# First-stage loads on a semaphore of their own, the first norm ahead of the table casts, the stack memsets at two bodies' ends

## What is computed

```python
x = L0_attn_x
x = x + _L0_attn_ref(_layernorm(x), W_in, W_out)      # q, k, v; clip; T_n(q), T_n(k); cumsum(T_n(k) v); num/den; @ W_out.T
x = x + _L0_ffn_ref(_layernorm(x), ln1_g, ..., exp_b2)

# inside _L0_ffn_ref
x = x + _attention(_layernorm(x, ln1_g, ln1_b), Wq, bq, Wk, bk, Wv, bv, Wp, bp)   # 16 heads, causal softmax
x = x + _token_moe(_layernorm(x, ln2_g, ln2_b), gate_W, gate_b, exp_W1, exp_b1, exp_W2, exp_b2)
```

## Time and profile before

| | us |
|---|---|
| median of 3 runs | 1512.45 (1511.88 to 1514.55) |
| the profiled execution | 1512.91 |
| its span | 1510.7 |
| PE busy | 1260.2 (83%) |
| DVE busy | 1167.6 (77%) |
| ACT busy | 918.9 (61%) |
| POOL busy | 854.2 (57%) |

### The profile page before, as it was taken

One profiled execution on the slowest core, in us unless ns is written; L12 is line 12 of the kernel. 1 busy time (PEld: TensorE's weight loads), 2 busy tenths in 40 slices (PEclk: granted clock), 3 DMA queues, 4 the chain that ended last, 5 costly groups with the idle time before them and its releaser, 6 DMA issues.

```text
span 1510.7 us, 27693 instructions
## 1 busy us (share of the span) xinstructions
PE 1260.2 (83%) x8757; PEld 722.4 (48%) x8819; DVE 1167.6 (77%) x2654; ACT 918.9 (61%) x1794; POOL 854.2 (57%) x1077
## 2 busy tenths in 40 slices
PE   2545898999989999998999999989888199999970
PEld 0222354544545454454544545444445178888850
DVE  4548789888998988889898898875551578888864
ACT  1131376666767667675666766666545289999950
POOL 5567445766676666656766666552032326666660
PEclk9666799999999999999999999999999589999995
DMA  3012321404223141321403214043143022222238
GB/s 97 0 49 36 85 64 23 103 20 107 65 51 86 30 112 50 67 79 37 110 21 92 75 34 100 16 100 86 30 135 134 30 76 77 86 86 81 81 134 333
DMA packets 79345, 116.23 MB, mean 77 GB/s; under 512 B 15396, under 2 KB 61496, under 8 KB 74976
## 3 DMA queue, kind: packets, MB, share of 16 engines
q1 hardware_dynamic: 65888, 92.41, 23.4%
q0 software_dynamic: 9088, 17.33, 3.4%
q10 hardware_dynamic: 4224, 4.72, 1.0%
HBM read 58.29 MB, written 57.43 MB: 77 GB/s over the span
## 4 chain that ended last, share of the span: by engine, by line
PE 61%; DVE 18%; issue 7%; ACT 6%; DMA 4%; POOL 3%; SPq 1%; POOLq 0%; DVEq 0%; another core or an unknown queue 0%; ACTq 0%
DVE nm L580 9%; PE scores L1386 8%; PE front L1547 7%; PE back L1406 7%; PE back L1559 7%; PE maxima L1360 7%; PE front L1289 3%; PE front L1264 3%; ACT pr L963 3%; PE scores L1389 2%; PE back L1243 2%; PE maxima L1362 2%; DMA stack<-pairs 2%; DVE front L531 1%; PE front L1338 1%
## 5 line engine op out<-in xcount | busy, mean ns | idle before, releaser
L580 DVE TENSOR_REDUCE nm<-maxima 128x1 f32<-128x384 f32 (+3 forms) x704 | 427.7, 634 | 94.1 <-PE maxima L1362 67.3
L963 ACT ACTIVATE pr<-scores 128x384 f32<-128x384 f32 (+1 forms) x768 | 378.5, 524 | 186.4 <-PE scores L1389 172.3
L1360 PE MATMUL maxima<-stack 96*128 96x128 bf16 (+3 forms) x1024 | 258.2, 311 | 43.1 <-DVE nm L580 33.2
L1386 PE MATMUL scores<-stack 98*128 98x512 bf16 (+3 forms) x1024 | 260.7, 310 | 33.7 <-ACT pr L963 27.8
L1386 PEld LDWEIGHTS scores<-stack 98*128 98x128 bf16 x1024 | 91.7, 101 | 205.6 <-ACT pr L963 134.1
L1389 PE MATMUL scores<-maskB,identb 128*128 128x128 bf16 (+1 forms) x768 | 186.4, 243 | 0.0
L1406 PE MATMUL back<-pr,vaug 128*9 128x512 f32 (+3 forms) x2048 | 183.2, 454 | 0.0
L1164 POOL DMA_INDIRECT xg<-rows,sloti x128 | 129.9, 1014 | 88.4 <-DVE sloti L653 47.0
L1134 POOL TENSOR_TENSOR kv<-F,kv 128x512 f32<-128x512 f32 x80 | 112.5, 1418 | 116.2 <-DVE kv L534 116.2
L1360 PEld LDWEIGHTS maxima<-stack 96*128 96x128 bf16 x1024 | 85.8, 99 | 169.1 <-DVE nm L580 113.4
L1232 POOL DMA_INDIRECT pairs<-xs x104 | 111.0, 1067 | 78.8 <-DVE xs L814 52.0
(11 more groups left out here) (223 smaller groups left out, 2491.7 us busy)
## 6 DMA issues: line engine op xcount, KB each, us to landing
stack<-spread SPq DMA_DIRECT2D x64, 384.0 KB, 6.4
spread<-qs SPq DMA_DIRECT2D x96, 128.0 KB
spread<-ks SPq DMA_DIRECT2D x96, 128.0 KB
xs<-xg SPq DMA_DIRECT2D x39, 272.0 KB, 2.9
stack<-pairs SPq DMA_DIRECT2D x8, 1024.0 KB, 16.6
xg<-xs SPq DMA_DIRECT2D x17, 272.0 KB
xs<-in_x SPq DMA_DIRECT2D x16, 256.0 KB, 5.8
acc<-xs SPq DMA_DIRECT2D x16, 256.0 KB, 2.3
```

The source lines that it names most:

```text
L580: v.tensor_reduce(nm[:, h:h + heads, t], ring(n)[:, 0:heads * (t + 1) * P].rearrange("p (h n) -> p h n", h=heads), AX.X, ALU.max, negate=T ...
L963: a.activation(pr[:, n % PR, 0:width], ringE[n % 2][:, 0:width], ACT.Exp).then_inc(W.exp_ready, 1)
L1360: k.matmul(ring(n)[:, at:at + (t + 1) * P], qst[p][0:MROW, h, t * P:(t + 1) * P], kst[p][0:MROW, h, 0:(t + 1) * P], start=(j == 0), stop=T ...
L1386: k.matmul(dst[:, at:at + T - t * P], kst[p][0:MROW + 2, h, t * P:(t + 1) * P], qst[p][0:MROW + 2, h, t * P:T], start=(t == tiles[0]), sto ...
```

## The change

The loads are split. `first_loads` (cst, w_in_sb, col) come right behind x of batch 0 and count on `f_loaded`; the nine others follow on `w_loaded`. The casts and tables move from before the loop into `set_tables`, which DVE runs behind the first norm's applies in body 0. The bias product moves to the end of body 0, as `add_bias` on DVE and `value_bias` on PE. ACT runs an activation of one column before it waits for the first loads, and waits for the other loads at the end of body 0. POOL sets stack buffer 0 at the end of body 0 and buffer 1 at the end of body 1, and SP waits for the pair that it is about to load.

```diff
-            loads = [(cst, consts[:, 0:C_KEPT]), (masks, consts[:, C_KEPT:C_N]), (col, cols), (row, row_biases), (w_in_sb, w_in),
-                     (wo_sb, w_out), (wq_sb, wq), (wk_sb, wk), (wv_sb, wv), (wp_sb, wp), (gw_sb, gate_w)]
+            first_loads = [(cst, consts[:, 0:C_KEPT]), (w_in_sb, w_in), (col, cols)]
+            loads = [(masks, consts[:, C_KEPT:C_N]), (row, row_biases), (wo_sb, w_out), (wq_sb, wq), (wk_sb, wk), (wv_sb, wv), (wp_sb, wp), (gw_sb, gate_w)]
             load_x(0)
+            for dst, src in first_loads:
+                sp.dma_start(dst[:, :], src).then_inc(W.f_loaded, 16)
...
-                    if g == 0:
-                        sp.wait_ge(W.stack_set, 4)
+                    if g < 2:
+                        sp.wait_ge(W.stack_set, 2 * g + 2)
...
-            dve.wait_ge(W.w_loaded, 16 * 12)
-            v.tensor_copy(identb[:, :], ident)
...
+            def set_tables():
+                dve.wait_ge(W.f_loaded, 16 * 3)
+                dve.wait_ge(W.w_loaded, 16 * 9)
+                v.tensor_copy(identb[:, :], ident)
...
+                v.tensor_scalar(bqs[:, :], col[:, V_BQ:V_BQ + 1], SCALE, None, ALU.mult).then_inc(W.const_ready, 1)
+            def add_bias():
+                dve.wait_ge(W.bp_step, 1)
+                v.tensor_copy(kv[:, 1, 0:D], X[:, 0:D]).then_inc(W.bp_step, 1)
+                dve.wait_ge(W.bp_step, 3)
+                v.tensor_tensor(row[:, R_BP:R_BP + D], X[:, 0:D], row[:, R_BP:R_BP + D], ALU.add).then_inc(W.bp_step, 1)
...
                     if at(17, f):
                         apply0(f)
+                        if f == 0:
+                            set_tables()
...
+                if f == 0:
+                    add_bias()
...
-            act.wait_ge(W.const_ready, 4)
-            act.wait_ge(W.w_loaded, 16 * 12)
+            act.wait_ge(W.const_ready, 1)
+            a.activation(warm[:, :], one[:, :], ACT.Copy)
+            act.wait_ge(W.f_loaded, 16 * 3)
...
+                if f == 0:
+                    act.wait_ge(W.const_ready, 4)
+                    act.wait_ge(W.w_loaded, 16 * 9)
...
-                if f == 0:
-                    for i in range(2):
-                        g_.memset(qst[i].rearrange("p h n -> p (h n)").bitcast(F32), 0.0).then_inc(W.stack_set, 1)
-                        g_.memset(kst[i].rearrange("p h n -> p (h n)").bitcast(F32), TWO_ONES).then_inc(W.stack_set, 1)
...
+                if f in (0, 1):
+                    g_.memset(qst[f].rearrange("p h n -> p (h n)").bitcast(F32), 0.0).then_inc(W.stack_set, 1)
+                    g_.memset(kst[f].rearrange("p h n -> p (h n)").bitcast(F32), TWO_ONES).then_inc(W.stack_set, 1)
...
-            pe.wait_ge(W.w_loaded, 16 * 12)
-            k.transpose(X[:, 0:D], row[:, R_BV:R_BV + D], ident).then_inc(W.bp_step, 1)
...
+            pe.wait_ge(W.f_loaded, 16 * 3)
+            def value_bias():
+                pe.wait_ge(W.w_loaded, 16 * 9)
+                pe.wait_ge(W.hq_ev, 1)
+                k.transpose(X[:, 0:D], row[:, R_BV:R_BV + D], ident).then_inc(W.bp_step, 1)
...
+                if f == 0:
+                    value_bias()
```

More of the change, by code:

```diff
@@ L262, in block_kernel @@
         names = """
-            bp_step stack_set w_loaded e_loaded const_ready pool_const tr0
+            bp_step stack_set f_loaded w_loaded e_loaded const_ready pool_const tr0
             h_taken hq_mm hk_mm hv_mm hk_ev hq_ev hv_ev k_clip q_clip k_sq q_sq k_t35 q_t35 k_t24 q_t24
@@ L473, in _ @@
             v.memset(vaug[:, :, :, :, DH:DH + 1], 1.0).then_inc(W.const_ready, 1)
-            dve.wait_ge(W.w_loaded, 16 * 12)
-            v.tensor_copy(identb[:, :], ident)
[L476 to L491, removed]
+            def set_tables():
+                dve.wait_ge(W.f_loaded, 16 * 3)
+                dve.wait_ge(W.w_loaded, 16 * 9)
+                v.tensor_copy(identb[:, :], ident)
+                v.tensor_copy(maskA[:, :].rearrange("p (h n) -> p h n", h=4), masks[:, 0:P].unsqueeze(1).to_broadcast((P, 4, P)))
+                v.tensor_copy(maskB[:, :].rearrange("p (i n) -> p i n", i=2), masks[:, P:2 * P].unsqueeze(1).to_broadcast((P, 2, P)))
+                v.tensor_copy(triu[:, :], masks[:, 2 * P:3 * P])
+                v.memset(onesb[:, :], 1.0)
+                v.tensor_copy(filled_to[:, :], cst[:, C_RG:C_RG + E])
+                v.memset(rows[:, :, :, D:RW], 0.0).then_inc(W.meta_ready, 1)
+                dve.wait_ge(W.meta_ready, 1)
+                v.tensor_copy(rowsi[:, :, :, R_ID], cst[:, C_TK:C_TK + 2 * QT].rearrange("p (k t) -> p k t", k=2)).then_inc(W.meta_ready, 1)
+                v.memset(fill, 0.0).then_inc(W.p_step, 1)
+                dve.wait_ge(W.p_step, 1)
+                v.tensor_copy(fill.rearrange("p (t c) -> p t c", t=QT)[:, :, R_ID].bitcast(U32), cst[:, C_DU:C_DU + QT]).then_inc(W.fill_ready, 1)
+                v.tensor_scalar(bqs[:, :], col[:, V_BQ:V_BQ + 1], SCALE, None, ALU.mult).then_inc(W.const_ready, 1)
@@ L1244, in turn @@
                 last.then_inc(done, 1)
-            pe.wait_ge(W.w_loaded, 16 * 12)
-            k.transpose(X[:, 0:D], row[:, R_BV:R_BV + D], ident).then_inc(W.bp_step, 1)
[L1248 to L1251, removed]
+            pe.wait_ge(W.f_loaded, 16 * 3)
[3 more added lines that the diff above has]
+                k.transpose(X[:, 0:D], row[:, R_BV:R_BV + D], ident).then_inc(W.bp_step, 1)
+                pe.wait_ge(W.bp_step, 2)
+                k.matmul(X[:, 0:D], kv[:, 1, 0:D], wp_sb[:, :], start=True, stop=True).then_inc(W.bp_step, 1)
+                pe.wait_ge(W.bp_step, 4)
+                pe.wait_ge(W.const_ready, 4)
             def turn_h(f, h, g):
```

## The result

Over 14 runs of each the changed kernel takes 1504.09 us (median) against 1512.01. The ratio is 0.9951 with a 95% interval of 0.9941 to 0.9962, so 5.7 to 8.9 us faster, 7.4 in the middle. 6.8 was forecast. The profiled execution took 1504.77 with a span of 1502.5, 8.2 shorter than before. One run, of 1590.97 us at a granted clock of 0.791 where the others have 0.909 to 0.916, is left out of the ratio.

What follows compares the result with a forecast made beforehand. Bound by a chain of single-instruction waits up to the first stack load, not throughput. 14.7 - 0.1 - 0.85 - 6.9 = 6.8 us off, forecast 1506.0 us; own range 1504.4 to 1508.5, 8 in 10 1502.8 to 1510.2.

Steps and rivals of the forecast that it cites:

- Start of the norm: Front of the kernel: first norm's statistics wait for x alone, at 3.8 in place of 17.18; gain 13.4 us.
- Table load: Prologue: a tiny ACT activation takes the table load at 24.01 off the chain before hT; gain 1.3 us.
- Tables and bias product: Body 0: tables hidden before the clip, cost nothing; bias product at the body's end delays PE's head sums, cost 0.1 us.
- TensorE's clock: Whole kernel: uncertainty; a matmul group on the other clock level moves the end by up to 1.7 us either way.
- First pair: POOL's memsets before the second norm's root: mostly covered, applies slower beside three POOL products; cost 0.85 us.
- Second pair: POOL's memsets before the root of norm 2, where DVE idles: nothing covers them, cost the full 6.9 us.
- products blocked: Rival at the first memsets: DVE's two-input products wait them out; 3.2 us lost, gain 4.4, 1508.5 us; chance 0.15.
- Stretched memsets: Rival at both pairs: memsets last longer among working engines; at 7 us each, slower at 1519 us; chance 0.07.
- The table load on the chain: Rival at ACT's start: the table load stays on the chain; gain 5.5 us, 1507.4 us; chance 0.04.
- The clock: Rival in the first bodies: two groups of ten fall to TensorE's lower level, 3.4 us lost, 1509.5 us; chance 0.12.

Runs made afterwards that it cites:

- memsets only: The kernel before with only POOL's four stack memsets moved to the ends of bodies 0 and 1; ratio to the kernel before 1.0005 (0.9991 to 1.0018).

## Why the prediction held

- Start of the norm: forecast 3.8, measured 3.52, because x landed after 2.7 us where the old trace had 3.0. hT at 10.35 for 10.6. This term was 0.25 short.
- Table load: 1.3 in the sum, 1.19 to 1.26 alone.
- Tables and bias product: the tables are hidden, as worked out. PE's head sums were released by DVE's bias add (ended 22.05) and not by POOL, and started at 22.33, 15.6 ahead of before where POOL's step was 15.8 ahead: 0.25 late where the sum has 0.1. None of it reached the chain, since DVE then waited for the root.
- TensorE's clock was named as the uncertainty and helped in body 0, which is luck and not part of the mechanism: the projections took 4.47 in place of 5.49, which put 0.9 on the lead by POOL's even orders. The head sums took 4.69 in place of 5.76, but that gain ended in DVE's wait for the root. Over the whole span the granted clock was lower than before, 0.913 against 0.917.
- First pair: forecast 0.85, measured 1.3 (15.84 to 14.51). The mechanism is the one worked out: DVE's products at 1.28, then applies of 3.95 beside three POOL products. What was missed is that the root's small steps stretch beside DVE's products. The first took 0.77 us in place of 0.22 and ended at 32.69, just behind the products (32.62), so the root came 0.55 later and DVE waited 1.57 for it. How much this costs depends on where the products fall: in the second trace of the changed kernel it is 0.2 and the pair costs 1.0 (15.59 to 14.57).
- Second pair: forecast 6.9, measured 6.90 (14.43 at DVE's step before POOL's last even orders, 58.31 against 72.74, to 7.53).
- Sum at the denominators of body 2: 14.95 at hT, +0.9 clock, -1.3 first pair, -0.1 on the way to 58.31, -6.9 second pair, which is 7.5. Forecast were 14.7 - 0.1 - 0.85 - 6.9 = 6.85. Without the lucky 0.9 it would be 6.6, so the forecast of 6.8 stands without it. The time of 1504.09 is 1.9 below the 1506.0 said: 0.9 of it can be this clock, 0.4 is the kernel before, which took 1512.01 over 14 runs where the three that I had gave 1512.45, and the rest was not traced. That the shift goes through to the end held (8.2 in the span), but not by all engines keeping one distance: in the loop it lay between 4.6 and 8.1.
- Rivals: products blocked, out (1.30 beside the memset). Stretched memsets, out (3.51 each). The table load on the chain, out. The clock gave 0.9 in front where the rival had it take 3.4.
- By the Trainium skill's page "SBUF — State Buffer", section "Who interferes with whom", a VectorE instruction with two SBUF inputs contends with a GpSimd instruction that reads SBUF and not with one that only writes it. The traces agree: two products took 1.30 us beside a memset and 6.73 beside a fill that reads. They also agree the other way round: the root's first step, which reads SBUF, ended only behind the two products. The prediction quoted the rule for the memsets and did not ask it of the root.

## What to carry to other kernels

While a pipeline fills, a step's price is what its neighbours wait at that place, so work that is moved off the first chain must be followed through the next two or three turns; here 14.95 us were won and half given back at one root. Where an engine has to set memory early, give it to the engine with the longest idle stretch, here ACT with 24 us: that was worth 7.2 and 8.7 us more at the denominators of body 2. Over the whole kernel the ratios (0.9882 and 0.9912 against 0.9951) put it at about 10 and 6 us. Parts of such a change don't add: measure each both as done alone and as undone alone.

## What the runs showed of the hardware

- A DVE clip in SBUF (0.43 us) that began 0.6 us before the end of a POOL memset waited through the next memset too, 4.33 us in all. Two casts of before got in between two memsets: they had waited since 9.13 and 9.27 and ended at 11.47 and 11.73, beside a memset that began at 11.32 and took 3.86 in place of 3.51. What decides between the two cases is not shown.
- A DVE product of two SBUF inputs took 6.13 us in place of about 0.69 beside a POOL tensor_scalar that reads SBUF, yet ended at 34.64, 1.2 us before that instruction's recorded end at 35.81, and the next product ran at its normal 0.69 inside it.
- A POOL step on 4 elements that reads SBUF took 0.77 us in place of 0.22 when it began beside DVE products of two SBUF inputs.
- ACT fills 128 x 4096 words from a broadcast column in 3.60 us, about as fast as POOL's memset (3.51).
- The kernel before ran at 1512 us on some chips and at 1551 on others. In the trace of "memsets only", from one of the latter, the first exponential stands at 181.7 (181.1 in the trace of before), the last at 1187.1 (1158.0), and the span is 1550.0 (1510.7). So some 28 of the 39 us are in the loop and 10 behind it. Its mean granted clock is 0.907 against 0.917; whether that is all of it is open.
